# One block in place of two: a graph kernel's normalisation and first layer joined

## What is computed

```python
def _layernorm(x, axis=-1, eps=1e-05):
    m = jnp.mean(x, axis=axis, keepdims=True)
    v = jnp.var(x, axis=axis, keepdims=True)
    return (x - m) / jnp.sqrt(v + eps)

def _L0_gnn_ref(features, edge_src, edge_dst, edge_weight, W, b):
    msgs = features[edge_src] * edge_weight[:, None]
    agg = jax.ops.segment_sum(msgs, edge_dst, num_segments=N_NODES, indices_are_sorted=True)
    return jnp.einsum('ni,oi->no', agg, W) + b
...
x = x + _L0_gnn_ref(_layernorm(x, axis=-1), src, dst, edge_weight, W, b)
x = x + _L0_ffn_ref(_layernorm(x, axis=-1)[None], ...)[0]
```

## Time and profile before

| | |
|---|---|
| median of 3 runs | 3662.67 us (3661.21 to 3663.2) |
| the profiled execution | 3665.02 us |
| its span (first to last instruction) | 3663.2 us |
| opening, up to the border | about 109 us |
| first gather from `feats` (L673) | 120.72 us |
| busy: PE, DVE, ACT, POOL | 2973.1, 2040.8, 819.5, 2708.5 us |
| granted TensorE clock, mean | 0.901 of full |

### The profile page before, as it was taken

One profiled execution on the slowest core, in us unless ns is written; L12 is line 12 of the kernel. 1 busy time (PEld: TensorE's weight loads), 2 busy tenths in 40 slices (PEclk: granted clock), 3 DMA queues, 4 the chain that ended last, 5 costly groups with the idle time before them and its releaser, 6 DMA issues. The chain is left out here.

```text
span 3663.2 us, 60252 instructions
## 1 busy us (share of the span) xinstructions
PE 2973.1 (81%) x13893; PEld 2429.7 (66%) x13894; DVE 2040.8 (56%) x6854; ACT 819.5 (22%) x2321; POOL 2708.5 (74%) x2817
## 2 busy tenths in 40 slices
PE   1475665666866889978889799999999999999748
PEld 1354444554645666656666688888888888888637
DVE  8777668787787676563443322443443344342567
ACT  6300000000110111212222222233232323232247
POOL 6677777777777777777777777777777777777673
PEclk6787877787877999999999899999999999999879
DMA  9643333333333444444444222242222222232279
GB/s 348 195 123 105 107 110 112 110 115 112 116 115 112 120 123 123 124 121 124 128 131 127 62 76 54 54 119 57 73 54 73 57 73 56 71 73 60 60 285 385
DMA packets 276697, 425.17 MB, mean 116 GB/s; under 512 B 59304, under 2 KB 210355, under 8 KB 275507
## 3 DMA queue, kind: packets, MB, share of 16 engines
q0 software_dynamic: 114208, 217.09, 23.4%
q1 hardware_dynamic: 64319, 114.73, 8.5%
q10 hardware_dynamic: 98004, 91.50, 7.7%
HBM read 317.12 MB, written 105.98 MB: 115 GB/s over the span
## 5 line engine op out<-in xcount | busy, mean ns | idle before, releaser
L673 POOL DMA_INDIRECT rows<-feats,src_t x1500 | 1453.7, 969 | 464.2 <-issue 444.7
L1202 POOL DMA_INDIRECT got<-row_dram,src_sorted x1024 | 990.8, 968 | 312.2 <-issue 312.2
L836 PE MATMUL node_sums<-rows,ys_ahead 128*128 x3904 | 989.2, 407 | 232.7 <-SPq L657 116.9
L836 PEld LDWEIGHTS node_sums<-rows,ys_ahead 128*128 128x128 f32 x3904 | 761.7, 202 | 428.7 <-issue 314.6
L1285 PE MATMUL d_hidden<-d_yt,w 128*128 128x256 f32 x3136 | 710.4, 380 | 0.8 <-DVE d_yt L1371 0.8
L1296 PE MATMUL d_expert<-w,hid 128*128 128x256 f32 x3136 | 708.7, 379 | 0.0
L1296 PEld LDWEIGHTS d_expert<-w,hid 128*128 128x128 f32 x3136 | 595.8, 190 | 81.0
L1285 PEld LDWEIGHTS d_hidden<-d_yt,w 128*128 128x128 f32 x3136 | 593.1, 190 | 80.1 <-DVE d_yt L1371 1.2
L1348 DVE TENSOR_TENSOR yo<-d_expert,x_and_b 128x512 f32<-128x512 f32 x196 | 135.6, 692 | 837.6 <-PE d_expert L1296 830.1
L895 DVE TENSOR_SCALAR ys_ahead<-iota,rel,ew_t 128x128 f32<-128x128 f32 x1952 | 557.2, 363 | 65.1 <-DVE rel L891 2.0
L1229 ACT ACTIVATE hid<-d_hidden,b1c 128x256 f32<-128x256 f32 x784 | 324.5, 472 | 979.6 <-PE d_hidden L1285 789.1
(11 more groups left out here) (305 smaller groups left out, 2277.7 us busy)
## 6 DMA issues: line engine op xcount, KB each, us to landing
y_dram<-yo ACTq DMA_DIRECT2D x196, 256.0 KB, 2.2
ys<-y_dram SPq DMA_DIRECT2D x36, 1024.0 KB, 9.2
rows<-feats,src_t POOLq DMA_INDIRECT x1500
got<-row_dram,src_sorted POOLq DMA_INDIRECT x1024, 2.4
ys_ahead<-y_dram SPq DMA_DIRECT2D x13, 1024.0 KB, 9.2
x_dram<-edge_plan ACTq DMA_DIRECT2D x98, 128.0 KB
d_x<-x_dram ACTq DMA_DIRECT2D x49, 256.0 KB, 3.0
ys_ahead<-in_x ACTq DMA_DIRECT2D x97, 128.0 KB
```

Of the source, the lines that this page charges most:

```text
L673: pool.indirect_dma_start(rows[:, g % RING, j, :], None, feats, bass.IndirectOffsetOnAxis(ap=m.src_t[:, g * GT + j:g * GT + j + 1], axis=0 ...
L836: t = pe.matmul(psA[:, ds(((code >> 1) & 1) * 512, FEAT)], hot[:, r, j, :], rows[:, ds((code >> 2) & (RING - 1), 1), j, :], start=False, s ...
L1202: pool.indirect_dma_start(got[:, k, j, 0:ROWF], None, m.row_dram, bass.IndirectOffsetOnAxis(ap=m.src_sorted[:, BEGIN[b] + j:BEGIN[b] + j + ...
```

## The change

`layernorm_and_plan` no longer opens a block. It returns its five programs, and part B's programs call them as their first piece, so that each engine goes from the opening into part B by itself. Where the border kept order, waits stand now:

- POOL waits for the chunk in buffer 7 before its constants (one lies in that buffer), and for all stores before the first gather from `feats`; ACT waits for buffer 7 before its first load of `x`; DVE for buffer 6 before its first one-hot matrices, and for buffers 4, 5 and 7 before the sort.
- The lent buffers are renamed so that the one-hot matrices lie where chunk 6 was, which no later chunk reuses (chunks 4 and 12 share buffer 4, 5 and 13 buffer 5).
- SP issues the loads of W, the attention vectors and the edge lists (`weights`) after the store of chunk 9, in place of after the border.
- Groups' readiness is counted by ACT directly (`rows_ready`), not relayed by SP.
- Small tensors of the opening move into free ends of `w1` and `w2`, and part B's PSUM lies over the opening's; PE waits for the plan (`PLANNED`) before it turns W.

```diff
+W_AFTER = 9
+PLANNED = 5
+HOT_SLOT, LO_SLOT, HI_SLOT, X_SLOT = 0, 1, 2, 3
+LO_CHUNK, HI_CHUNK, HOT_CHUNK, X_CHUNK = 4, 5, 6, 7
...
     q = act.activation(m.rows[:, g, j, :], ...)
-    q.then_inc(m.s_gn, 1)
+    q.then_inc(m.s_ready, 1)
...
         own = [m.ys_ahead[:, q].rearrange("p t e f -> p (t e f)")[:, 0:CH * FEAT].rearrange("p (t f) -> p t f", f=FEAT)
-               for q in range(XB - 2 * LENT)]
+               for q in (LO_SLOT, HI_SLOT, HOT_SLOT, X_SLOT)]
...
-        block = ctx.enter_context(nc.Block(no_gpsimd_drain=True))
-
-        @block.sync
-        def _(sp):
+        def sync(sp, weights):
...
                 if 1 <= n <= CHUNKS - XB:
                     sp.wait_ge(s_out[n - 1], 16)
                     load(n - 1 + XB)
+                if n == W_AFTER:
+                    sp.wait_ge(s_ev, PLANNED)
+                    weights(sp)
             for k in range(XB):
                 sp.wait_ge(s_out[k], m.stores[k])
...
-            v.wait_ge(s_norm, CHUNKS)
-            v.wait_ge(m.s_gn, PRE_DONE)
...
+            pe.wait_ge(s_ev, PLANNED)
+
+        return sync, gpsimd, scalar, vector, tensor
...
+        def stored(eng, *slots):
+            for k in slots:
+                eng.wait_ge(m.s_store[k], m.stores[k])
...
         @block.sync
         def _(sp):
-            for g in range(PRE_DONE):
-                sp.wait_ge(m.s_gn, g + 1)
-                sp.sem_inc(s_ready, 1)
...
+            open_sync(sp, weights)
...
             sp.wait_ge(s_pc, PC)
+            sp.wait_ge(s_ready, RING)
...
             c = Count(pool, s_pc)
+            open_gpsimd(pool)
+            pool.wait_ge(m.s_ev, PLANNED)
+            stored(pool, X_CHUNK)
             c.inc(pool.memset(zero_b[:], 0.0))
...
             assert c.n == PC
+            stored(pool, *range(m.XB))
             for g in range(RING, GROUPS):
                 refill(g)
...
+            open_scalar(act)
             act.sem_inc(s_evac, 1)
+            stored(act, X_CHUNK)
             load(0, 0)
...
+            open_tensor(pe)
             pe.wait_ge(s_wr, 16)
...
                 v.wait_ge(s_ei, 32)
+                stored(v, LO_CHUNK, HI_CHUNK, X_CHUNK)
...
+            open_vector(v)
+            stored(v, HOT_CHUNK)
             for r in range(XS):
                 one_hots(r, r, first=True)
```

More of the change, by code:

```diff
@@ L1 @@
+import math
 from contextlib import ExitStack
@@ L159, in build @@
             m.s_gst, m.s_gvar, m.s_gstd = sem("a_group_stats"), sem("a_group_var"), sem("a_group_std")
-            m.s_grcp, m.s_gscale, m.s_gn = sem("a_group_reciprocal"), sem("a_group_scale"), sem("a_group_normed")
-            layernorm_and_plan(nc, sem, x, src, dst, edge_weight, feats, m)
-            weighted_sums(nc, sem, feats, edge_index, x, W, b, W_gat, att_src, att_dst, W1, b1, W2, b2, m)
+            m.s_grcp, m.s_gscale = sem("a_group_reciprocal"), sem("a_group_scale")
+            m.s_ready = sem("rows_ready")
+            opening = layernorm_and_plan(nc, sem, x, src, dst, edge_weight, feats, m)
+            weighted_sums(nc, sem, opening, feats, edge_index, x, W, b, W_gat, att_src, att_dst, W1, b1, W2, b2, m)
         attention_and_experts(nc, sem, m)
@@ L198, in group_normalise, with beside_x @@
                            scale=m.g_mv[:, g, j, 1:2], bias=m.g_shift[:, g, j:j + 1])
-    q.then_inc(m.s_gn, 1)
+    q.then_inc(m.s_ready, 1)
 def layernorm_and_plan(nc, sem, x, src, dst, ew, feats, m):
     with ExitStack() as ctx:
-        def sb(name, shape, dt):
-            return ctx.enter_context(nc.sbuf_tensor(name, shape, dt))
-        XB = 8
+        XB = m.XB = 8
         LENT = 2
         own = [m.ys_ahead[:, q].rearrange("p t e f -> p (t e f)")[:, 0:CH * FEAT].rearrange("p (t f) -> p t f", f=FEAT)
-               for q in range(XB - 2 * LENT)]
-        xlast = sb("x_last", [P, FEAT], F32)
+               for q in (LO_SLOT, HI_SLOT, HOT_SLOT, X_SLOT)]
+        beside = {}
+        def beside_x(a, *shape):
+            flat = a[:].rearrange("p a b c -> p (a b c)")
+            n = math.prod(shape)
+            at = beside.get(a.name, LENT * CH * FEAT)
+            beside[a.name] = at + n
+            assert at + n <= flat.shape[1]
+            return flat[:, at:at + n]
+        xlast = beside_x(m.w1, FEAT)
         lent_w = [a[:].rearrange("p a b c -> p (a b c)")[:, q * CH * FEAT:(q + 1) * CH * FEAT].rearrange(
@@ L216, in layernorm_and_plan @@
         xin = lent_w + own
[L217 to L220, removed]
+        stats = beside_x(m.w2, XB, CH, 6).rearrange("p (k t c) -> p k t c", t=CH, c=6)
+        mv = beside_x(m.w2, XB, CH, 2).rearrange("p (k t c) -> p k t c", t=CH, c=2)
+        rstd = beside_x(m.w2, XB, CH).rearrange("p (k t) -> p k t", t=CH)
+        shift = beside_x(m.w1, XB, CH).rearrange("p (k t) -> p k t", t=CH)
         raw_i = m.rows[:].rearrange("p r t f -> p (r t f)")[:, (RING - 4) * GT * FEAT:(RING - 4) * GT * FEAT + 2 * ECOLS
@@ L225, in layernorm_and_plan @@
         raw_f = spent[:].rearrange("p (a b e) -> p a b e", a=3, e=P)
-        last_sel = sb("last_sel", [P, P], F32)
+        last_sel = beside_x(m.w1, P)
         part = m.node_row[:].rearrange("p t c -> p (t c)")
@@ L231, in layernorm_and_plan @@
         odd = m.seg_keep[:, STEPS:2 * STEPS].bitcast(I32)
-        gend = sb("gend", [P, 4], F32)
+        gend = beside_x(m.w1, 4)
         passed = spent[:, 0:4 * STEPS].rearrange("p (q s) -> p q s", q=4)
@@ L247, in layernorm_and_plan @@
         s_pl = sem("a_pool")
+        m.s_ev = s_ev
         s_edge = sem("a_edge_vector")
@@ L332, in _, with scalar @@
                                             ).then_inc(m.s_got[g], 16)
-        @block.scalar
-        def _(act):
+        def scalar(act):
             act.wait_ge(s_raw0, 3)
@@ L365, in _, with vector @@
                 group_deviation(act, m, g)
-        @block.vector
-        def _(v):
+        def vector(v):
             c = Count(v, s_edge)
@@ L431, in plan_steps @@
                 c.done(v.tensor_tensor(m.step_code[:], m.step_code[:], last[:], ALU.bitwise_or))
+                v.sem_inc(s_ev, 1)
             v.wait_ge(s_raw[0], 3 * 16)
@@ L459, in _, with tensor @@
                 group_scale(v, m, g)
-            v.wait_ge(s_norm, CHUNKS)
-            v.wait_ge(m.s_gn, PRE_DONE)
-        @block.tensor
-        def _(pe):
+        def tensor(pe):
             pe.wait_ge(s_const, 5)
@@ L488, in spread, with weighted_sums @@
                             m.node_dst[:, t, :], None).then_inc(m.s_sc, 16)
-def weighted_sums(nc, sem, feats, edge_index, x, W, b, W_gat, att_src, att_dst, W1, b1, W2, b2, m):
+def weighted_sums(nc, sem, opening, feats, edge_index, x, W, b, W_gat, att_src, att_dst, W1, b1, W2, b2, m):
     XS = 4
@@ L518, in weighted_sums @@
         rel = sb("rel", [P, XS, GT])
-        hot = m.ys_ahead[:, 0].rearrange("p t e f -> p (t e f)").rearrange("p (r j n) -> p r j n", j=GT, n=P)
+        open_sync, open_gpsimd, open_scalar, open_vector, open_tensor = opening
+        hot = m.ys_ahead[:, HOT_SLOT].rearrange("p t e f -> p (t e f)").rearrange("p (r j n) -> p r j n", j=GT, n=P)
         key = [m.seg_keep[:], m.src_sorted[:].bitcast(F32), lent(GCOLS)]
@@ L533, in weighted_sums @@
         sums_t = lent(FEAT)
-        xs = m.ys_ahead[:, 3].rearrange("p t e f -> p (t e f)")[:, 0:XS * FEAT].rearrange("p (r f) -> p r f", f=FEAT)
+        xs = m.ys_ahead[:, X_SLOT].rearrange("p t e f -> p (t e f)")[:, 0:XS * FEAT].rearrange("p (r f) -> p r f", f=FEAT)
         x1 = lent(2 * FEAT).rearrange("p (h f) -> p h f", f=FEAT)
@@ L562, in weighted_sums @@
         s_ei = sem("b_edge_index")
-        s_ready = sem("b_rows_ready")
+        s_ready = m.s_ready
         s_got = m.s_got
@@ L622, in _ @@
             sp.dma_start(key_i[1], edge_index[0, :].rearrange("(p j) -> p j", p=P)).then_inc(s_ei, 16)
-            for g in range(PRE_DONE, RING):
-                sp.wait_ge(m.s_gn, g + 1)
-                sp.sem_inc(s_ready, 1)
+        @block.sync
+        def _(sp):
+            open_sync(sp, weights)
             def expert_load(k):
```

12 lines of the change are left out of this document (5 added, 7 removed).

## The result

The changed kernel takes 3652.82 us (median of 11 runs, 3650.53 to 3653.9), the kernel before 3662.67 us in the same comparison: a ratio of 0.9971, with a 95% interval of 0.9962 to 0.998. The forecast was 3653.5 in a range of 3651.3 to 3657.3.

A forecast was written before the change was run, and what follows sets the result against it. POOL's unbroken gather stream was taken to bound the kernel. PE's earlier first step moves the first gather from `feats` from 120.72 to 111.53, 9.2 us, bringing the median from 3662.67 to 3653.5 us, range 3651.3 to 3657.3.

The forecast's parts named there:

- What bounds: POOL's stream of 1500 gathers in part B sets the end, a fixed time behind the first gather from `feats`.
- ACT's copy, PE's opening, first product: Start of part B: W's copy ends at 105.32 instead of 114.51, PE opens at 105.48, first product at 106.95.
- Step 0 at the 1.2 GHz level, 3.78 us: PE's first step in part B keeps clock 0.50 and takes 3.78 us, ending at 110.73.
- POOL's constants and DVE's one-hot matrices, at no cost: Before PE's first product: constants end at about 103.4, matrices at 104.4, 3.5 and 2.5 us early; cost nothing.
- SP's seven issues: Early loads on SP's queue: 0.43 us each, 3 us in all, fitting between two stores; upper bound 3.08 each.
- the choked queue: Rival: seven issues at 3.08 us each delay SP's stores, first gather at 133.9, 3675.8 us; chance 0.03.
- The way from the last landing to the gather: On POOL, reading the group's end (1.05) and starting (0.80) put the first gather 1.85 us behind the last store's landing.
- The last store's landing: End of the opening: early loads delay it by 0, upper bound 3.5 us; landing at 108.7 allows the gather at 110.5.
- The rival of the longer stores: Rival: unabsorbed early loads land the last store at 112.2, gather at 114.05, gain 6.7, 3656.0 us; chance 0.10.
- The sum: First gather from `feats` at 111.53 instead of 120.72, 9.2 us earlier; median 3653.5 us, 0.25% less.
- The gain given back in the middle: Rival: around 1178 us PE and DVE come late against POOL; one slow PE step gives 3655.4, two 3657.3; chance 0.14.

The follow-up runs named there:

- pool_plus10_b: The changed kernel with 18 clearing writes on POOL, some 10.5 us in all, between its constants and its first gather from `feats`; 3663.4 us.
- border_kept: The changed kernel, but POOL, ACT, DVE and PE wait behind their opening until SP has seen every store; early loads stay; 3660.32 us.
- loads_late: The changed kernel, but SP issues W, the vectors and the edge lists behind the last store; the border stays open; 3658.46 us.
- edges_late: The changed kernel, but the two edge lists (1 MB) are issued behind the stores; W and the small vectors stay early; 3652.28 us.
- steps_first: edges_late, with PE's waits for W and the copy of the turned W moved behind its first four steps; 3650.66 us.
- best_b: steps_first, with the statistics of groups 10 and 11 moved on DVE from the opening into part B; 3651.12 us.
- dve_late14_b: The changed kernel with 25 extra writes on DVE in its unit 14 of the first layer, 13.0 us; 3666.62 us.
- dve_late26_b: The changed kernel with the same 25 extra writes on DVE in its unit 26, past its sort; 3652.18 us.

## Why the prediction was right, and where it was not

The rule, held against every profile of these chips but that of pool_plus10_b, where the added writes stand between the landing and the gather. The 1.87 is from the changed kernel's profile and the 0.80 from that of before; the other rows test them. Landing is the issue of the last store plus the time of its row; all in us.

| kernel | last store lands | + 1.87 | PE ends step 0 | + 0.80 | first gather |
|---|---|---|---|---|---|
| before | 108.8 | 110.7 | 119.92 | 120.72 | 120.72 |
| changed | 110.6 | 112.5 | 110.69 | 111.49 | 112.50 |
| border_kept | 109.1 | 111.0 | 118.71 | 119.51 | 119.52 |
| loads_late | 110.0 | 111.8 | 117.88 | 118.68 | 118.69 |
| edges_late | 108.9 | 110.8 | 110.45 | 111.25 | 111.25 |
| steps_first | 109.1 | 110.9 | 108.88 | 109.68 | 110.94 |
| best_b | 108.2 | 110.1 | 109.11 | 109.91 | 110.06 |
| dve_late14_b | 109.8 | 111.6 | 110.59 | 111.39 | 111.65 |
| dve_late26_b | 109.4 | 111.3 | 110.33 | 111.13 | 111.27 |

**What bounds.** That the end lies a fixed time behind the first gather was right: 10.75 us there were 10.6 at the end.

**ACT's copy, PE's opening, first product.** Forecast 104.73, 105.48 and 106.95; measured 104.75, 105.36 and 106.94. Right. What fills the 1.47 us between PE's opening and its first product no row shows: DVE's first matrices were ready well ahead of it, and it measured 1.58 here and 1.49 in border_kept and loads_late.

**Step 0 at the 1.2 GHz level, 3.78 us.** Forecast end 110.73, measured 110.69. PE's granted clock reads 0.50 up to 110.5, 0.87 in 110 to 112 and 1.00 from 112, when the step was over:

```profile
109.00:110.50 1.50, 1.50 (x5) 1.16 (x4) 1.40 (x6) 1.50 (x4) 0.00 (x0) 0.50 0.06 22
...
110.00:112.00 2.00, 2.00 (x9) 1.67 (x8) 1.97 (x10) 2.00 (x5) 0.00 (x0) 0.87 0.05 15
```

**POOL's constants and DVE's one-hot matrices, at no cost.** The constants run from 98.98 to 102.59, the first matrices are ready at 104.2, both ahead of 106.9. Right.

**SP's seven issues.** I took 0.43 each, 3 us; they took 4.7, still between two stores, and the stores of chunks 10 to 13 were issued within 0.15 us of their old times. At no cost, as forecast; the choked queue did not come.

**The way from the last landing to the gather.** Forecast 1.85 (1.05 and 0.80), measured 1.87. Right, though the 1.05 was taken from another engine.

**The last store's landing, "I take 0": this term failed, and with it the gate.** Its upper bound was 3.5. In the changed kernel's profile the store landed 1.8 us later than before, which made the stores the gate and cost 1.0 us at the first gather: 112.50 for 111.53. My words were that the stores allow the gather 1.0 before PE and are "next"; they were first. I had also priced the loads' transfer at nothing because the store follows 20 us later (16 as it ran) and the shares in between left room; but the loads, which carry 1.25 MB, kept the share at 0.94 to 1.06 from 88 up to 104 (it had been 0.58 at the end of this stretch), and the stores of chunks 10 and 11 landed 7 to 8 us later than before. The rival of the longer stores happened at half its size.

The size scatters: two more profiles with the same opening (dve_late14_b, dve_late26_b) have the last store 4.5 and 4.2 us after its issue, and first gathers at 111.65 and 111.27, and pool_plus10_b has 5.7. The mean of the four is 4.95. Without early lists it is 3.7 before, 3.6 and 3.7 in edges_late and steps_first, but 4.0 in loads_late and 4.2 in best_b, so the lists' share in the 1.8 us is less certain than their effect on chunk 10. ACT's loads of `x` may have a part in it. ACT issues the second once the first has landed: with early lists that is at 104.1 to 104.8, right beside the last stores; in edges_late it is 2.6 us earlier than in the changed kernel:

```profile
102.11 0.36 ACTq L743 DMA_DIRECT2D ys_ahead<-in_x  x1
```

border_kept has the early lists without a load of `x` in this stretch, and its last store takes 3.9; edges_late and steps_first have these loads without the lists, and take 3.6 and 3.7. The 4.2 to 5.7 us came where both were there. How much each delays is not shown.

The row of 109.0 to 110.5 above shows what the mean share hides: while the last store was still on its way, the share was 0.06, as much as one of the 16 DMA engines gives by itself (1/16). So at the end there was no backlog on all of them; by this estimate the landing waited for one that was behind.

The rule of the Trainium skill, DMA: Bandwidth & Descriptors, section "Issuing engines are not separate DMA queues", that all transfers share the same 16 engines, was what I had weighed against the trace's spare share. The trace agrees with the rule rather than with my reading of the share: SP's lists delayed ACT's load as well (its second is issued at 104.70 with them, at 102.11 without).

**The sum.** 8.2 us at the first gather in place of 9.2, and 9.85 by the medians. The missing 1.0 is made up by about 1.6 that the head does not explain. Every one of the kernels but dve_late14_b has such a surplus over before, between 0.4 us (edges_late: 9.9 by the medians, 9.5 at the gather) and 1.7, pool_plus10_b included (0.8 slower where the gather is 2.5 later). There is one profile of the kernel before, so whether its start or its length is untypical can't be told. Its gathers add up to 1453.7 us, those of the nine other profiles on these chips, border_kept among them, to 1447.2 to 1450.3, which points at the length. Where the surplus comes from is open; the forecast hit its number within 0.7 partly by luck: the missing 1.0 at the gather and the surplus stand against each other.

**The gain given back in the middle (0.14).** It did not happen in the changed kernel: POOL's 40 later waits on PE are at the usual gap. My reading of the earlier trace rows was off, though. The gather at 1178.15 has PE as its releaser, but the one that PE's step 236 frees is the next, at 1179.44, and that step had ended 1.64 us earlier. In the changed kernel the distance is 2.21, so it did not shrink with the earlier start, as the forecast had argued. In the eight profiles without a stall it lies between 1.2 and 3.5, of which 0.79 is the way; what is left is small and differs from one execution to the next. In best_b PE ended step 236 at 1057.9 us behind the first gather, against 1053.8 in the changed kernel and 1057.1 before the change, and POOL stalled for 2.7 us. One profile can't tell whether its earlier start or the scatter did that; steps_first, which starts 1.6 us earlier than the changed kernel, did not stall. What is shown is that delays of DVE ahead of this place are lost in full once the small room is gone (13.0 us cost 13.8).

## What to carry to other kernels

Neither opening the border nor loading early paid much by itself (2.0 and 1.2 us at the first gather) and both together paid 8.2: price such edits by the later of the gates, not one by one. A transfer put ahead of stores in their own queue is not free because the DMA share leaves room later: the stores behind it land late, and where the next wait is for the last of them, its landing has to be priced. A mean share over 16 engines need not show that one of them is behind. After each gain, look for what is next; here it was first the last store, and then, in one profile, a sort 1060 us further on.

## What the runs showed of the hardware

- Two lists of 512 KB each, issued ahead of a store of 896 KB in the same queue, took its landing from 5.2 us after issue to 12.3, 7.1 us more (10.7 to 12.3 in four profiles, 4.4 to 5.5 in five without them), although at the 345 to 394 GB/s of 92 to 100 us their own transfer is an estimated 2.7 to 3.0 us.
- From a landing that POOL waits for, over its register read, to the gather takes 1.87 us (five profiles), and 0.80 where only PE's semaphore is left (four). In none of the five does the gather's row name the store: it names PE or nothing.
- While the last store of the changed kernel was still on its way, from 109.0 to 110.5, the DMA share was 0.06.
- On one chip the kernel before took 6152 us in place of 3663, with POOL waiting for PE up to 36.3 us at a time. The four kernels tried there lie within 0.12% of it, none clear of the noise.
